# Routing weights into the expert activations, experts cut in chunks across their borders

## The reference

```
x = x + attn0(layernorm(x), ctx);  x = x + ffn0(layernorm(x))
x = x + attn1(layernorm(x), ctx, indices);  x = x + ffn1(layernorm(x))

ffn0:  scores = sigmoid(x @ gate.T + bias);  top 2 of 9, normed -> cw[t, e]
       out = sum over e of cw[:, e] * ((silu(x @ w1[e].T) * (x @ w3[e].T)) @ w2[e].T)       9 experts of 352
ffn1:  probs = softmax(x @ gate_w.T);  top 2 of 8, normed -> combine[t, e]
       out = sum over e of combine[:, e] * ((silu(x @ w_gate[e]) * (x @ w_up[e])) @ w_down[e])   8 experts of 176
       out += sigmoid(x @ shared_gate) * (shared expert of 176)
```

## Time and profile before

| | us |
|---|---|
| median of 3 runs (lowest, highest) | 1637.76 (1637.12, 1640.99) |
| the profiled execution | 1640.13, its span 1638.3 |
| PE busy | 1456.4 (89%) |
| DVE busy | 1169.3 (71%) |
| ACT busy | 787.7 (48%) |
| POOL busy | 620.8 (38%) |
| mean granted TensorE clock | 0.94 of full speed |

### The profile page before, as it was taken

The page is one execution under the profiler, slowest core; times in us unless marked ns, Lnnn a source line. Parts: engine busy times, 40 slices in busy tenths (PEclk is TensorE's granted clock), DMA queues, the critical chain, the costliest instruction groups (busy, mean ns, idle before and its releaser), DMA issues.

```text
span 1638.3 us, 34256 instructions
## 1 busy us (share of the span) xinstructions
PE 1456.4 (89%) x12878; PEld 838.2 (51%) x12878; DVE 1169.3 (71%) x2574; ACT 787.7 (48%) x1200; POOL 620.8 (38%) x1081
## 2 busy tenths in 40 slices
PE   2289998999988998989989998999989899889967
PEld 2133365347633575336743476435753367336836
DVE  4078477868777687867777687777778587885554
ACT  1246624772266623754257722765247532666231
POOL 0425513681057412573046611564136620452030
PEclk9589989999999999989999999989999899999967
DMA  7230300022000310012100210004100210000000
GB/s 221 51 66 20 94 19 2 21 54 62 1 2 30 74 33 1 11 43 56 29 2 21 74 42 1 11 22 77 29 1 21 51 37 4 2 2 16 4 1 4
DMA packets 64853, 53.65 MB, mean 33 GB/s; under 512 B 14762, under 2 KB 57140, under 8 KB 64692
## 3 DMA queue, kind: packets, MB, share of 16 engines
q1 hardware_dynamic: 64692, 51.47, 12.9%
HBM read 38.98 MB, written 12.46 MB: 31 GB/s over the span
## 4 chain that ended last, share of the span: by engine, by line
PE 69%; DVE 14%; POOL 5%; ACT 5%; issue 4%; SPq 1%; DMA 1%; POOLq 0%; ACTq 0%
PE ob L615 11%; PE um L680 10%; PE um L669 10%; PE um L670 8%; PE um L602 6%; PE um L587 6%; DVE mx L1032 4%; PE um L565 3%; DVE big L1137 3%; ACT probs L855 2%; DVE mx L1141 2%; PE um L654 2%; PE um L731 1%; PE um L757 1%; PE um L540 1%
## 5 line engine op out<-in xcount | busy, mean ns | idle before, releaser
L1032 DVE TENSOR_REDUCE mx<-um 128x2 f32<-128x802 f32 (+1 forms) x512 | 504.2, 989 | 129.0 <-PE um L587 125.1
L855 ACT ACTIVATE probs<-um 128x1024 f32<-128x1024 f32 (+1 forms) x448 | 426.6, 962 | 226.2 <-PE um L602 219.1
L861 ACT ACTIVATE hid<-um 128x256 f32<-128x256 f32 (+1 forms) x328 | 125.4, 382 | 422.1 <-PE um L670 421.9
L615 PE MATMUL ob<-probs,vaug 128*9 128x256 f32 (+1 forms) x3328 | 288.8, 397 | 0.9 <-ACT oT L831 0.6
L1215 POOL TENSOR_TENSOR big<-iotab,idx_lo 128x512 bf16<-128x512 bf16 x256 | 277.4, 1101 | 31.1 <-PE um L757 24.4
L587 PE MATMUL um<-kst,qa 64*128 64x401 bf16 (+1 forms) x1024 | 177.4, 348 | 25.9 <-ACT probs L855 8.8
L602 PE MATMUL um<-big,kst 64*128 64x256 bf16 (+1 forms) x1664 | 175.8, 285 | 27.0 <-DVE mx L1141 18.0
L1178 POOL CAST qst<-nm 128x4 bf16<-128x4 f32 x64 | 19.3, 301 | 449.8 <-DVE nm L1038 449.7
L1044 DVE TENSOR_TENSOR hid<-hid,um 128x256 f32<-128x256 f32 (+1 forms) x328 | 135.5, 414 | 45.4 <-ACT hid L861 42.6
L669 PE MATMUL um<-xnT,w1T 128*128 128x256 f32 (+1 forms) x432 | 139.1, 404 | 0.0
L670 PE MATMUL um<-xnT,w3T 128*128 128x256 f32 (+1 forms) x432 | 129.1, 381 | 0.0
(11 more groups left out here) (208 smaller groups left out, 2147.9 us busy)
## 6 DMA issues: line engine op xcount, KB each, us to landing
kst<-k_parts SPq DMA_DIRECT2D x384, 50.0 KB
k_parts<-big SPq DMA_DIRECT2D x72, 128.0 KB, 1.9
ctx_sb<-in_ctx SPq DMA_DIRECT2D x8, 768.0 KB
k1st<-k_parts SPq DMA_DIRECT2D x96, 32.0 KB
k_parts<-big SPq DMA_DIRECT2D x24, 64.0 KB, 2.9
kst<-in_L_ffn_w SPq DMA_DIRECT2D x1, 1408.0 KB
x<-in_x SPq DMA_DIRECT2D x8, 128.0 KB, 4.0
out<-x SPq DMA_DIRECT2D x8, 128.0 KB, 2.0
```

Source lines behind the costliest of these rows:

```text
L615: m = pe.matmul(ob[q:q + V1, 0:NQ], vaug[b % 2][0:kn, c, 2 * p + hh, :], probs[0:kn, (2 * (NGB * b + g) + hh) % NPS, (c % 2) * NQ:(c % 2 + ...
L855: act.activation(probs[0:kn, k:k + 2, 0:w], own_banks, ACT.Exp).then_inc(f_read, 1)
L861: act.activation(hid[0:nr, own % NHID, :], quarter[place[ev][0]][0:nr, 0:NQ], ACT.Silu).then_inc(th_ready, 1)
L1032: dve.tensor_reduce(mx[:, p % 2, s, :, j], pair[:, :, 0:w], AX, ALU.max, negate=True).then_inc(u_read, 1)
```

## The change

- **The routing weight is applied before the down product.** A new piece `cm` multiplies `hid` on DVE, 128 x 256 fp32, all in SBUF, by a tile `cwb` that has the weight of each token in its columns, the same row on every partition of one expert.
- **The weights get there through DRAM.** `ct0` and `ct1`: after routing PE transposes `cw[l]` (9 rows x 256), DVE copies it to SBUF, SP stores it to `cw_rows` in DRAM; `cl`: SP waits for the store and loads it back, one row spread over the partitions of its expert, in 12 tiles (19 DMAs) for layer 1 and 15 tiles (21 DMAs) for layer 0 a batch, into five buffers of 128 x 256 fp32 (1 KB a partition). A load waits until the product that used its buffer is done.
- **Chunks cross expert borders**: the hidden units of all nine experts are one row of 3168 or 1584, cut into 25 and 13 chunks of 128. A chunk that holds two experts has its weight tile in two DMAs.
- **One sum in PSUM a layer.** The down product is done by chunk (`dk`, two matmuls) and summed over all chunks of a layer in the second half of `ob`. DVE adds it to x once a layer (`acc`). `w0` of the next batch, which starts sums in the same bank, waits for `acc`; so does the first `dk` of a layer.
- **The numbers in the list**: `hid` has 6 buffers instead of 8. R is 87.34 units. Layer-1 experts start at 56.34, layer-0 experts at 65.59. Early `part`s start at 57.37 (before 54.27) with 1.139 units between (1.05); the later ones are due about 6 units later, the last at 43.1 (37.1). `rel` 0 to 2 at 46.1, `rel` 3 at 64.0, the last `key` of the long row at 37.0 (38.4). Around the borders of the stages the order is now:

The chunks gu0 to gu24 are layer 0 and gu25 to gu37 layer 1. The diff, cut to its core:

```diff
-NHID = 8
+NHID = 6
+NCW = 5
+        cwT = [oT[0:NE, :], sb("cwT1", [P, NQ])[0:NE, :]]
+        cwb = sb("cwb", [P, NCW, NQ])
+        acc = ob[:, NQ:2 * NQ]
...
+                put(own + XL + AT["ct0"], "ct0", b)
-                for u in range(len(chunk0)):
+                for u in range(NC0):
                     put(own + Y0 + CL * u, "gu", b, u)
                     put(own + Y0 + CL * u + AT["hd"], "hd", b, u)
-                for e in range(NE):
-                    put(own + Y0 + CL * (J0 * e + 2) + AT["dn0"], "dn", b, e)
+                    put(own + Y0 + CL * u + AT["cm"], "cm", b, u)
+                    put(max(own + Y0 + CL * u + AT["dk0"], own + Y1 + C1 * (NC1 - 1) + AT["dk1"] + 0.3 + 0.01 * u), "dk", b, u)
...
 @block.sync
+                elif kind in ("ct0", "ct1"):
+                    l = int(kind[-1])
+                    sp.wait_ge(u_read, rel[ev] + 1)
+                    if b >= 1:
+                        sp.wait_ge(hw_ready, users["cl", b - 1, (len(tiles), NT_L1)[l] - 1])
+                    sp.dma_start(cw_rows[l], cwT[l]).then_inc(cw_out, 16)
+                elif kind == "cl":
+                    l, own, _ = tiles[n]
+                    k = turn[ev]
+                    if n in (0, NT_L1):
+                        sp.wait_ge(cw_out, 16 * count[f"ct{l}", b, 0])
+                    if k >= NCW:
+                        sp.wait_ge(hw_ready, users[cl_order[k - NCW]])
+                    for e, r0, r1 in own:
+                        sp.dma_start(cwb[r0:r1, k % NCW, :], cw_rows[l, e, :].partition_broadcast(r1 - r0)).then_inc(cwb_in[k % NCW], 16)
 @block.tensor
-            def down(b, e):
+            def down(b, u):
+                l, c = layer(u)
+                n = chunk_rows(u)
+                own = turn["dk", b, u]
+                pe.wait_ge(hw_ready, own + 1)
+                if c == 0:
+                    if own == 0:
+                        pe.wait_ge(pre_dve, 11)
+                    else:
+                        pe.wait_ge(acc_read, acc_before["dk", b, u])
+                    pe.wait_ge(oT_ready, w0_before["dk", b, u])
                 for s in range(NS):
...
+                    m = pe.matmul(acc[:, s * P:(s + 1) * P], hid[0:n, own % NHID, s * P:(s + 1) * P], (w2T, wd_sb)[l][0:n, c, :],
+                                  start=(c == 0 and s == 0), stop=(c == (NC0, NC1)[l] - 1), skip_group_check=True)
+                m.then_inc(dn_done, 1)
...
+                elif kind in ("ct0", "ct1"):
+                    bank = free_bank(ev)
+                    l = int(kind[-1])
+                    pe.wait_ge(cw_ready, count[ev])
+                    for s in range(NS):
+                        m = pe.transpose(bank[0:NE, s * P:(s + 1) * P], cw[l][:, s, :], ident[:, :])
+                    m.then_inc(m_psum, 1)
 @block.vector
-                elif kind == "dn":
...
+                elif kind == "cm":
+                    own, nr = turn[ev], chunk_rows(n)
+                    cl = "cl", b, tile_of[n]
+                    k = turn[cl] % NCW
+                    dve.wait_ge(cwb_in[k], 16 * loads[cl])
+                    dve.wait_ge(u_read, rel["gu", b, n] + 1)
+                    h = hid[0:nr, own % NHID, :]
+                    dve.tensor_tensor(h, h, cwb[0:nr, k, :], ALU.mult).then_inc(hw_ready, 1)
+                elif kind == "acc":
+                    dve.wait_ge(dn_done, 1 + turn["dk", b, NC0 - 1 if n == 0 else NCH - 1])
+                    dve.tensor_tensor(X[:, :, :], acc.rearrange("p (s d) -> p s d", s=NS), X[:, :, :], ALU.add).then_inc(acc_read, 1)
+                elif kind in ("ct0", "ct1"):
+                    dve.tensor_copy(cwT[int(kind[-1])], bank[0:NE, 0:NQ]).then_inc(u_read, 1)
```

More of the change, by code:

```diff
@@ L268, in last_down, with layer, owners @@
-        def last_down(own):
-            b, u = divmod(own, NCH)
-            return "dn", b, max(e for e in range(2 * NE) if u in [piece[0] for piece in down_pieces(*divmod(e, NE))])
+        NCH = NC0 + NC1
+        WIDTH = (I0, I1)
+        def layer(u):
+            return (0, u) if u < NC0 else (1, u - NC0)
+        def chunk_rows(u):
+            l, c = layer(u)
+            return rows(c, F0) if l == 0 else P
+        def owners(u):
+            l, c = layer(u)
+            first, last = c * P // WIDTH[l], min((c * P + P - 1) // WIDTH[l], NE - 1)
+            if first == last:
+                return [(first, 0, P)]
+            cut = last * WIDTH[l] - c * P
+            return [(first, 0, cut), (last, cut, P)]
@@ L273, in build @@
+        tiles, tile_of = [], {}
+        for u in list(range(NC0, NCH)) + list(range(NC0)):
+            if len(owners(u)) == 1 and tiles and tiles[-1][0] == layer(u)[0] and tiles[-1][1] == owners(u):
+                tiles[-1][2].append(u)
+            else:
+                tiles.append((layer(u)[0], owners(u), [u]))
+            tile_of[u] = len(tiles) - 1
+        NT_L1 = sum(1 for t in tiles if t[0] == 1)
         F_NEED = {"s0": 1, "s1": 1, "ctx": 1, "key": 1, "val": 1, "lat": 1, "kv1": 1, "all0": 1, "all1": 1, "w1": 1}
@@ L364, in build @@
         EV = order()
+        turn, users, loads = {}, {}, {}
+        for kind in ("gu", "hd", "cm", "dk", "cl", "acc"):
+            for k, ev in enumerate(v for v in EV if v[0] == kind):
+                turn[ev] = k
+        for ev in EV:
+            if ev[0] == "cm":
+                assert turn[ev] == turn["gu", ev[1], ev[2]] == turn["hd", ev[1], ev[2]] == turn["dk", ev[1], ev[2]]
+                users["cl", ev[1], tile_of[ev[2]]] = turn[ev] + 1
+        cl_order = [ev for ev in EV if ev[0] == "cl"]
+        slot_count = [0] * NCW
+        for k, ev in enumerate(cl_order):
+            slot_count[k % NCW] += len(tiles[ev[2]][1])
+            loads[ev] = slot_count[k % NCW]
+        acc_before, w0_before = {}, {}
+        nacc, nw0, summing = 0, 0, False
+        for ev in EV:
+            if ev[0] == "acc":
+                nacc += 1
+            elif ev[0] in ("dk", "w0", "out", "n2"):
+                acc_before[ev] = nacc
+            nw0 += ev[0] == "w0"
+            if ev[0] == "dk":
+                w0_before[ev] = nw0 // NG
+            if ev[0] == "dk":
+                assert summing == (layer(ev[2])[1] > 0) and nw0 % NG == 0
+                summing = layer(ev[2])[1] < (NC0, NC1)[layer(ev[2])[0]] - 1
+            assert ev[0] != "w0" or not summing
         fill, slot, rel, place, u_free, serial = {}, {}, {}, {}, {}, {}
@@ L610, in weigh @@
                     pe.wait_ge(oT_ready, NP * b + p)
+                if g == 0 and acc_before["w0", b, g] >= 1:
+                    pe.wait_ge(acc_read, acc_before["w0", b, g])
                 for c in chunks(j):
```

151 lines of the change are left out of this document (62 added, 89 removed).

## The result

Four runs of the changed kernel have a median of 1660.56 us (1659.53 to 1663.96), four of the kernel before beside them 1639.25: ratio 1.0134, 95% interval 1.0113 to 1.0156.

A forecast was written before the change was run, and what follows sets the result against it. PE was taken as the bound, full in the expert stage. Terms -40 - 7 + 14 + 4 + 15 + 21 - 17 = -10 us gave 1628 us against a median of 1637.8; own range 1613 to 1643, with rivals 1592 to 1668.

The forecast's parts named there:

- Moved maxima: Some five early row maxima a batch go from expert to attention stage: -7 us, between -14 and +7.
- PE work: Expert stage: fewer gate/up and down matmuls, less added weight transposes, net -5.0 us a batch, -40 us in eight.
- the end of the stage: End of expert stage: PE's waits of 3.6 us fall to about 1.2, -17 us over seven (0 to -25).
- Layer 1, transpose: PE waits 2.0 us (0 to 3) for routing before transposing layer 1's weights: +14 over seven, about +4 last batch.
- Layer 1, first product: PE waits 2.2 us before transposing attention's result, behind DVE's first product by loaded weights: +15 us over seven.
- Layer 0: PE waits 2.6 us (1.3 to 3.9) for row maxima and the layer-1 sum behind the weights' trip: +21 us in eight.
- DVE 64 to 67 us in the expert stage: DVE's busy time in the expert stage after the change, in a stage of 77 us: not the bound by its sum.
- Slower rival: Layer-1 store waits behind SP's key reload, PE waits about 5 instead of 2.2 us, clock drops: 1660 us, chance 0.30.
- The test I set: Forecast wrong altogether if expert stage under 74 or over 84 us, or attention, held at 111, moves over 2 us.

The follow-up runs named there:

- the late half: Second half of layer 0's row maxima, 5 groups later: alone on the kernel before 1664.35 us, ratio 1.0131; put back in the changed kernel 1662.13, 1.0121.
- the last experiment: Changed kernel, layer 0's routing sent sooner, its first products queued later, late maxima put back, plus layer 1's transpose behind its first chunk: 1631.03 us, ratio 0.9965.
- the first experiment: The changed kernel with every order value that both kernels have put back to the old one, except layer 1's start: 1701.99 us, ratio 1.0367.

## Why the prediction was wrong, by its steps

- *Moved maxima, -7, between -14 and +7*: **this is the step that failed.** I priced five maxima by what a record costs PE in either stage, took off 7 us for them (that switching mostly costs nothing in attention stood on no row), and held attention at 111. Measured, attention is 3.1 us longer a batch, 22 us over seven: 29 us from my term, of the 31 between forecast and result. With the places of all maxima put back it is 4.9 us a batch shorter, so it is the maxima that do it. I looked at DVE's sum over the stage and at whether each maximum still came before its user. I did not look at which PE rows lose their filler, nor at PE having to wait for a maximum on DVE, now 1.9 us a batch before the score matmuls where it was 0.3. Which half of the maxima does it in the changed kernel stays open: the late half put back takes 0.9 us a batch off, the early half alone was not put back. On the old sum the late half costs 1.0131 by itself, but 12 of these 21 us are a wait that the changed kernel doesn't have. Nor does the order explain the net time alone: on the new sum the old maxima made the gate and the experts longer by as much as attention got shorter.
- *PE work, -40, and the end of the stage, -17*, with the transpose's +18: -39 forecast. Measured with no trip waited for, and in the new order on both sides: -43. Close. The end, answering:

```profile
841.46 0.39 PE L655 MATMUL um<-big,kst 64*128 64x256 bf16 x4 [0.34 <-DVE big L1127]
842.37 0.34 PE L640 MATMUL um<-kst,qa 64*128 64x398 bf16 x2 [0.51 <-DVE mx L1098]
...
844.22 0.61 PE L655 MATMUL um<-big,kst 64*128 64x256 bf16 x4 [0.90 <-DVE mx L1098]
...
846.26 0.66 PE L587 MATMUL um<-ident,xn 128*128 128x128 f32 x2 [0.46 <-DVE xn L991]
```

0.34 + 0.51 + 0.90 + 0.46 = 2.2 left of 3.6, where I had 1.2: -1.4 a batch instead of -2.4.
- *Layer 1, transpose, 2.0*: 1.13 us in every batch. Low part of its bounds, and by the last experiment no separate cost.
- *Layer 1, first product, 2.2, +15 us*: 1.1 to 1.3 us before attention's transposes (772.58) in six of seven batches, 2.3 in the other. The kernel that doesn't wait for its trips has 0.84 us there too, so the trip owns only some 0.3, and layer 1 gives back 5.6 us in all. Too large: the trip is 4.7 us where I had 5.1 with SP's delay, which in most batches was none.
- *Layer 0, 2.6 (1.3 to 3.9), +21 us*: the waits are there (0.81, 0.47 and 2.75 us, then a clock of 0.60 for 4.3 us), and without them the stage is 3.8 to 6.6 us shorter, 4.8 as a mean of six: 3.5 of idle PE, and 1.2 by which PE is busy longer, at the lower clock. Over the eight stages and what is around them that is 37 us. Too small, and I had left the clock at 0. Together the trips of products cost 44 where I had 15 + 21 = 36, with the shares of the two layers far apart from mine.
- *DVE 64 to 67 us in the expert stage*: 18.46 + 40.41 = 58.9 in the batch shown, less than I had, and no bound by its sum, as I said; in attention it went from 77.4 to 85.1, which I did not work out.
- *Slower rival (layer-1 store behind the key reload, 1660)*: its number came true, and in the changed kernel its cause did not. In the batch shown the store issues 0.44 us after the copy's start. One batch has a layer 1 of 24.9 us, 2.5 more than the others; there the reload's issue ends at 573.02, the store follows at 573.11 and the product at 578.61, a trip of 5.5 instead of 4.7 us. But the mechanism is real: in the first experiment, with the keys at their old places, it is there in all six full batches, and layer 1 is 5 to 10 us longer (1.7 of it also in the kernel with the maxima alone put back). That fits my sentence that the new order does the last key product earlier, though that value was not timed alone.
- The test I set, attention moving by more than 2 us, was the one that struck.

## What to carry to other kernels

When an edit comes with a new order, time the order alone on the old arithmetic, the old order on the new, and the arithmetic with its waits taken away: here +21, -43 and +44 us were hidden in one +22, and the same order that cost the old sum 21 us saved the new one about 40. Look at every queue before you name the cause of such a gain: it was SP's, in which a small store stood behind twelve key loads. A periodic filler (a maximum every 1.2 groups) is to be judged by the rows of the other engine that it covers and the queue it stands in, not by the stage's sum of busy time. A wait on a transfer in an in-order queue costs what stands behind it: put other work ahead, and send the transfer off sooner; each gave half.

## What the runs showed of the hardware

- Broadcast loads of one row of device memory over partitions land in 2.7 us for 16 KB and 3.4 for 128 KB; a plain 128 KB store takes 2.0. The Trainium skill (DMA: Bandwidth & Descriptors, "Anatomy of one DMA") has about 2.0 us of fixed cost for a DMA, measured for those that GpSimd issues; the smallest load here, issued by SP, is 0.7 above it.
- SP issues in order: a 9 KB store that was ready at 581.07 left at 584.76, behind twelve loads whose issue took 4.12 us.
- Behind 12.4 us in which PE stood 4.0, the last 2.75 of them in one piece, the granted clock was 0.60 over 4.3 us of full work, and 1.00 after it.
- The same attention stage, in one kernel and in turn from batch to batch, took 111.1 us at a granted clock of 0.91 and 107.1 at 0.98, the longer one with *less* idle of PE (12.2 against 14.5 us). A stage can't be priced from one batch.
